# Graph layers on one Trainium2 core: 64x64 graph matrices, made a round ahead, and the values product in four quadrants

## What is computed

```python
# layer 0: attention, 8 heads of 64
attn = softmax(q @ k.T / 8) * 0.33 + 0.33 * adj + 0.33 * exp(-adj)      # masked
x = layernorm(x + (attn @ v) @ W_out + b_out)
# layer 1: mean over neighbours
agg = (adj @ x) / max(deg, 1e-6)
x = layernorm(x + relu(concat([x, agg]) @ W.T))
# layer 2: hypergraph convolution, twice, with H = (adj != 0)
Dn = 1 / (H @ adj[0]);  Be = 1 / H.sum(0)                               # 0 where the sum is not > 0
G = Dn * (H @ (Be * H.T));  h = layernorm(relu(G @ x @ W1.T + b1)) * gamma + beta
x = layernorm(x + G @ (h @ W2.T) + b2 + x)
# layer 3: gated attention
xg = x * sigmoid(deg * Wd + bd);  QK = sigmoid(xg @ Wqk.T + bqk)
s = (QK @ QK.T) / 16 * adj;  s = s / (s.sum(-1) + 1e-6)
x = layernorm(x + relu(s @ xg @ Wl.T + bl + xg @ Wr.T))
```

## Time and profile before

| | us |
|---|---|
| median of 3 runs (range) | 1361.08 (1360.6 to 1361.57) |
| the profiled execution, its own time | 1359.72 |
| its span, first to last instruction | 1357.9 |
| TensorE matmul busy | 1243.5 (92%), 11728 instructions |
| TensorE weight loads busy | 1074.6 (79%) |
| VectorE busy | 959.6 (71%), 2115 instructions |
| ScalarE busy | 551.9 (41%), 1058 instructions |
| GpSimd busy | 499.2 (37%), 633 instructions |
| granted TensorE clock, mean | 0.986 of full |

### The profile page before, as it was taken

One profiled execution on the slowest core, in us unless ns is written; L12 is line 12 of the kernel. 1 busy time (PEld: TensorE's weight loads), 2 busy tenths in 40 slices (PEclk: granted clock), 3 DMA queues, 4 the chain that ended last, 5 costly groups with the idle time before them and its releaser, 6 DMA issues.

```text
span 1357.9 us, 30718 instructions
## 1 busy us (share of the span) xinstructions
PE 1243.5 (92%) x11728; PEld 1074.6 (79%) x11728; DVE 959.6 (71%) x2115; ACT 551.9 (41%) x1058; POOL 499.2 (37%) x633
## 2 busy tenths in 40 slices
PE   5699999999999999999999999999999999999776
PEld 4578888788888878887888888878888887888665
DVE  4787676777767677776777777677776767777653
ACT  2344353443534344353444435344353534335221
POOL 2325252442624234261433525244262424425130
PEclk9899999999999999999999999999999999999897
DMA  6000101001010100101010010100101010010000
GB/s 199 21 20 21 36 2 40 15 19 35 11 44 0 39 15 19 35 0 39 15 39 15 19 35 0 39 15 20 34 19 35 0 39 19 0 36 2 20 1 16
DMA packets 43873, 34.93 MB, mean 26 GB/s; under 512 B 19319, under 2 KB 38717, under 8 KB 43838
## 3 DMA queue, kind: packets, MB, share of 16 engines
q1 hardware_dynamic: 43112, 34.04, 8.1%
q10 hardware_dynamic: 726, 0.40, 0.2%
HBM read 26.05 MB, written 8.39 MB: 25 GB/s over the span
## 4 chain that ended last, share of the span: by engine, by line
PE 63%; DVE 22%; issue 9%; ACT 4%; DMA 1%; DVEq 0%; POOL 0%; SPq 0%; ACTq 0%; POOLq 0%
PE bank L891 15%; PE bank L892 14%; PE bank L893 14%; PE bank L1067 5%; DVE x L681 4%; DVE hT_lo L605 3%; PE bank L984 3%; PE bank L959 3%; PE bank L1125 2%; DVE stats L670 2%; PE bank L1011 2%; PE bank L887 2%; DVE smax L713 2%; DVE x L822 2%; DVE yw L833 1%
## 5 line engine op out<-in xcount | busy, mean ns | idle before, releaser
L411 POOL TENSOR_SCALAR var<-mv 128x2 f32<-128x2 f32 (+1 forms) x192 | 42.5, 221 | 683.0 <-DVE mv L674 683.0
L681 DVE TENSOR_SCALAR x<-x,mv,rstd 128x256 f32<-128x256 f32 x256 | 129.7, 553 | 30.0 <-POOL rstd L414 29.9
L503 ACT ACTIVATE hT_hi<-bank 128x512 fp32r<-128x512 f32 x160 | 88.7, 600 | 142.6 <-PE bank L1011 116.2
L414 POOL TENSOR_TENSOR rstd<-var,negh 128x2 f32<-128x2 f32 (+1 forms) x192 | 127.1, 662 | 16.0
L605 DVE TENSOR_TENSOR hT_lo<-bank,hT_hi 128x512 fp32r<-128x512 f32 x160 | 102.9, 683 | 35.0 <-ACT hT_hi L503 30.6
L515 ACT ACTIVATE v<-bank 64x256 f32<-64x256 f32 x256 | 96.8, 378 | 56.5 <-PE bank L893 53.5
L670 DVE BATCH_NORM_STATS2 stats<-x 128x6 f32<-128x256 f32 x256 | 96.4, 419 | 4.4
L520 ACT ACTIVATE prob<-prob 128x512 f32<-128x512 f32 x64 | 40.5, 633 | 127.7 <-DVE prob L715 127.7
L456 POOL TENSOR_TENSOR prob<-prob,srec 128x512 f32<-128x512 f32 x64 | 66.8, 1044 | 65.5 <-DVE srec L723 65.5
L503 ACT ACTIVATE qT<-bank 128x512 f32<-128x512 f32 x64 | 38.3, 598 | 129.0 <-PE bank L893 129.0
L670 DVE BATCH_NORM_STATS2 stats<-r 128x6 f32<-128x512 f32 x64 | 44.5, 695 | 57.2 <-ACT r L503 57.2
(11 more groups left out here) (206 smaller groups left out, 3932.9 us busy)
## 6 DMA issues: line engine op xcount, KB each, us to landing
xTin<-in_x_t SPq DMA_DIRECT2D x32, 256.0 KB, 2.9
xin<-in_x SPq DMA_DIRECT2D x16, 512.0 KB, 3.7
out_x<-x SPq DMA_DIRECT2D x32, 256.0 KB, 2.3
adjA<-in_adj SPq DMA_DIRECT2D x16, 128.0 KB, 2.7
adjB<-in_adj SPq DMA_DIRECT2D x32, 64.0 KB, 3.0
r<-in_wqkv SPq DMA_DIRECT2D x2, 512.0 KB, 9.1
x<-in_wqkv SPq DMA_DIRECT2D x1, 512.0 KB, 10.7
x<-in_w_out SPq DMA_DIRECT2D x1, 512.0 KB, 11.0
```

The costliest lines, as they stand in the source:

```text
L414: pool.tensor_tensor(rstd[layer][:, lo:hi], var[layer][:, lo:hi], negh[:, lo:hi], ALU.pow).then_inc(SEM[f"rstd{n}"], 1)
L503: act.activation(dst, src[:, :], func, **kw).then_inc(SEM[ready], 1)
L681: ins = dve.tensor_scalar(x[:, t, :], x[:, t, :], mv[layer][:, t, 0:1], rstd[layer][:, t:t + 1], ALU.subtract, ALU.mult)
```

## The change

- The graph matrices are compact: 128 partitions (two graphs) x 4 tiles x 64 columns, half the elements, no zeros. adj is loaded as such, its transpose (adjAt, made ahead of the launch) and the first row of each graph spread over its partitions (wrow) too. Products on them are made in 64x64 squares (or 64 rows x 128 columns in `gathered`), one for each half of the partitions; `gathered` now makes both chunks in one step and fills both banks together, ordered by half.
- hT comes from adjAt by a comparison on VectorE; the counts and Dn's sums are reductions on VectorE. TensorE's graph_a and graph_b and ScalarE's graph_a are gone. The three transposes of the graph matrices and turn_s are products with the identity (`flipped`).
- All graph steps are now stream A's, in the middle and late part of the round, for the group that B takes up in the next round.
- pv takes two tiles in one step: even head pairs go straight into one bank, odd head pairs crosswise into the other, so that all four quadrants are used. W_out's rows are laid out to match.
- The banks are dealt out anew by the same rule.

```diff
-    ("B", "turn1", 0), ("B", "turn1", 1), ("A", "k", 1), ("B", "graph_a", 0), ("C", "scale3", 0), ("A", "k", 2),
+    ("B", "turn1", 0), ("B", "turn1", 1), ("A", "k", 1), ("C", "scale3", 0), ("A", "k", 2), ("A", "mask", 0),
...
-                    sp.wait_ge(*count("meanA_ready", b, 1, 1))
                     sp.wait_ge(*count("sim_ready", b, 1, 1))
-                    for h in range(2):
-                        sp.dma_start(adjB[h * N:(h + 1) * N, :, h * N:(h + 1) * N],
-                                     adj_h[b, h]).then_inc(SEM["adjB_in"], 16)
+                    sp.dma_start(adjB[:, :, :], adj_g[b]).then_inc(SEM["adjB_in"], 16)
...
             def graph_a(g, i):
 
-                dve.wait_ge(*count("adjB_in", g, 32))
-                dve.tensor_scalar(edge[:, :, :], adjB[:, :, :], 0.0, None, ALU.not_equal).then_inc(SEM["edge_ready"], 1)
-                dve.tensor_reduce(deg[:, :], adjB[:, :, :], AX.X, ALU.add).then_inc(SEM["deg_ready"], 1)
+                dve.wait_ge(*count("adjA_in", g, 16))
+                dve.wait_ge(*count("z_ready", g, 1, 1))
+                dve.tensor_reduce(deg[:, :], adjA[:, :, :], AX.X, ALU.add).then_inc(SEM["deg_ready"], 1)
+                dve.wait_ge(*count("adjAt_in", g, 16))
+                dve.tensor_scalar(hT0[:, :, :], adjAt[:, :, :], 0.0, None, ALU.not_equal).then_inc(SEM["ht_ready"], 1)
                 dve.wait_ge(*count("deg_ready", g, 1))
                 dve.tensor_scalar(degm[:, :], deg[:, :], 1e-6, None, ALU.max).then_inc(SEM["degmax"], 1)
+                dve.wait_ge(*count("ht_ready", g, 1))
+                dve.tensor_reduce(cnt[:, :], hT0[:, :, :], AX.X, ALU.add).then_inc(SEM["cnt"], 1)
...
             def graph_b(g, i):
...
+                dve.wait_ge(*count("cnt", g, 1))
+                dve.tensor_scalar(cntm[:, :], cnt[:, :], 1.0, None, ALU.max).then_inc(SEM["cntmax"], 1)
+                dve.wait_ge(*count("wrow_in", g, 32))
+                dve.scalar_tensor_tensor(out=edgew[:, :, :], in0=adjA[:, :, :], scalar=0.0, in1=wrow[:, :, :],
+                                         op0=ALU.not_equal, op1=ALU.mult).then_inc(SEM["edgew"], 1)
                 dve.wait_ge(*count("cntmax", g, 1))
                 dve.reciprocal(be[:, :], cntm[:, :]).then_inc(SEM["be_ready"], 1)
+                dve.wait_ge(*count("edgew", g, 1))
+                dve.tensor_reduce(dsum[:, :], edgew[:, :, :], AX.X, ALU.add).then_inc(SEM["dsum"], 1)
...
             def pv(g, i):
-                pe.wait_ge(*count("pT_ready", g, i + 1))
-                pe.wait_ge(*count("v_ready", g, i + 1))
...
+                if i % 2:
+                    return
+                pe.wait_ge(*count("pT_ready", g, i + 2))
+                pe.wait_ge(*count("v_ready", g, i + 2))
+                for odd in range(2):
+                    pe.wait_ge(*emptied("oT", i + odd, g))
+                    apart(pe, g)
+                ins = [None, None]
+                for k in range(2):
+                    for pair in range(HP // 2):
+                        for gr in range(2):
+                            for odd in range(2):
+                                p = 2 * pair + odd
+                                col = (pair * 2 + k) * P + gr * N
+                                for e in range(2):
+                                    rows, to = slice(e * N, (e + 1) * N), (e + odd) % 2
+                                    ins[odd] = pe.matmul(bank_of("oT", i + odd)[to * N:(to + 1) * N, col:col + N],
+                                                         v[rows, i + k, gr, p, :], pT[rows, k, p, gr * N:(gr + 1) * N],
+                                                         start=True, stop=True, skip_group_check=True)
...
+            def flipped(name, g, src):
+
+                pe.wait_ge(*emptied(name, 0, g))
+                dst = bank_of(name, 0)
+                apart(pe, g)
                 for t in range(T):
+                    for h in range(2):
+                        ins = pe.matmul(dst[square(h), t * N:(t + 1) * N], src[square(h), t, :],
+                                        ident[square(h), square(h)], start=True, stop=True, skip_group_check=True)
+                now_full(ins, name, 0)
...
+            def gathered(name, g, src, mat, halves=None):
+
+
+                ins = [None, None]
+                for c in range(C):
+                    for t in range(T):
+                        if halves and c == 0 and t % 2 == 0:
+                            pe.wait_ge(*count(halves, g, t // 2 + 1))
+                        at = slice((c * T + t) * N, (c * T + t + 1) * N)
+                        for h in range(2):
+                            if c == 0 and t == 0:
+                                pe.wait_ge(*emptied(name, h, g))
+                            ins[h] = pe.matmul(bank_of(name, h)[:, at], src[square(h), t, c * P:(c + 1) * P],
+                                               mat[square(h), t, :], start=True, stop=True, skip_group_check=True)
+                for h in range(2):
+                    now_full(ins[h], name, h)
...
                 now_full(product(dst[:, :], [(tile_of(spT, c, i), chunk(w1, c)) for c in range(C)], (0, HID),
-                                 [count("spread_lo", g, c + 1) for c in range(C)]), "up", i)
+                                 [count("spread_lo", g, 2)] * C), "up", i)
```

More of the change, by code:

```diff
@@ L89 @@
     "mixmat": "mm_ready", "q": "q_ready", "k": "k_ready", "v": "v_ready", "pT": "pT_ready", "oT": "oT_lo",
-    "out0": "sum0_ready", "turn1": "turn1_lo", "agg": "agg_lo", "mean": "sum1_ready", "ht": "ht_ready",
-    "cnt": "dsum", "sym": "g_ready", "meanT": "meanT_ready", "gT": "gT_ready", "spread": "spread_lo",
+    "out0": "sum0_ready", "turn1": "turn1_lo", "agg": "agg_lo", "mean": "sum1_ready", "sym": "g_ready", "meanT": "meanT_ready", "gT": "gT_ready", "spread": "spread_lo",
     "up": "relu_ready", "turn_h": "hT_lo", "down": "down_ready", "hyper": "sum2_ready", "turn3": "turn3_lo",
@@ L184, in graph_layers, with two @@
         rdeg = sb("rdeg", [P, T])
[L185 to L189 removed]
+        def two(name):
+            pair = sb(name, [P, 2, T, N])
+            return pair, pair[:, 0], pair[:, 1]
+        pair_m, meanA, meanT = two("mean")
+        pair_h, hT0, bhT = two("hyperedge")
+        cnt = sb("cnt", [P, T])
         cntm = sb("cntm", [P, T])
+        be = sb("be", [P, T])
         dsum = sb("dsum", [P, T])
[L192 to L194 removed]
         dsafe = sb("dsafe", [P, T])
@@ L211, in graph_layers @@
         xg = yw
-        sim = hT0
+        pair_s, sim, sT = two("sim")
         smat = sim
-        sT = bhT
+        lend = sb("lend", [P, 2 * HID + P])
         simsum = sb("simsum", [P, T])
@@ L282, in filled @@
             n = g * PER_BANK[b] + (c + 1 - back * PER_BANK[b])
-            return (zero_ready, 4) if isinstance(n, int) and n <= 0 else (full[b], n)
+            return (zero_ready, 2) if isinstance(n, int) and n <= 0 else (full[b], n)
         def emptied(fill, i, g):
@@ L642, in other_weights @@
                 if i == 2:
-                    three_parts([row0p[:, :, k] for k in range(3)], row0, gmat[:, 0, 0:T * GRP],
-                                gT[:, 0, 0:T * GRP])
                     dve.wait_ge(t_full, 1)
@@ L1054, in graph_d @@
-                dst = bank_of("gT", 0)
-                for t in range(T):
-                    ins = pe.transpose(dst[:, t * P:(t + 1) * P], gmat[:, t, :], ident[:, :])
-                now_full(ins, "gT", 0)
-            def gathered(name, g, i, src, mat, halves=None):
-                pe.wait_ge(*emptied(name, i, g))
-                dst = bank_of(name, i)
-                for t in range(T):
-                    if halves and i == 0 and t % 2 == 0:
-                        pe.wait_ge(*count(halves, g, t // 2 + 1))
-                    ins = pe.matmul(dst[:, t * P:(t + 1) * P], src[:, t, i * P:(i + 1) * P], mat[:, t, :],
-                                    start=True, stop=True)
-                now_full(ins, name, i)
+                flipped("gT", g, gmat)
@@ L1121, in simi @@
                 dst = bank_of("sim", 0)
+                apart(pe, g)
                 for t in range(T):
                     for c in range(C):
-                        tile = qkT[:, c, t * P:(t + 1) * P]
-                        ins = pe.matmul(dst[:, t * P:(t + 1) * P], tile, tile, start=(c == 0), stop=(c == C - 1))
+                        for h in range(2):
+                            one = qkT[:, c, t * P + h * N:t * P + (h + 1) * N]
+                            ins = pe.matmul(dst[square(h), t * N:(t + 1) * N], one, one, start=(c == 0),
+                                            stop=(c == C - 1), skip_group_check=True)
                 now_full(ins, "sim", 0)
@@ L1143, in out3 @@
                           + [(tile_of(agg3, c, t), chunk(wlr, c)) for c in range(C)], (HID + D, HID + 2 * D),
-                          [count("agg3_lo", g, c + 1) for c in range(C)])
+                          [count("agg3_lo", g, 2)] * C)
             steps = {
```

242 lines of the change are left out of this document (106 added, 136 removed), and 23 rows, old and new, of the table SCHEDULE.

## The result

The changed kernel takes 1544.66 us (median of 4 runs, 1541.84 to 1545.36), the kernel before 1360.84 beside it: ratio 1.1347, 95% interval 1.1327 to 1.1367. It is slower by 184 us. The direction was forecast, the size (+67) was not, and 1545 lies far outside the range of 1370 to 1455.

A forecast was written before the change was run, and what follows sets the result against it. TensorE is busiest, but VectorE, partly delayed by GpSimd, sets parts of the round. Dependence adds 2.0 us and the low clock 2.9: 14 x 4.9 = 69; with the ends, 1359.7 + 68 = 1428 us, range 1370 to 1455.

The forecast's parts named there:

- The first stretch: Round start to turn_h: mask product 4.1 us earlier, at 7.9; turn_h at 31.5 instead of 35.6.
- the prediction's 1.76: Gather agg3 at the round's end: 32 instructions take 1.76 us, counted equal to now (1.7).
- the load row: Trace row for weight loads: 192 ns for 128 columns, 137 for 64; used against faster gathers.
- The middle and pv 0: From turn_h to yw: hT0 waits for GpSimd's gate sum; TensorE stops 4.1 us, pv 0 at 44.15 against 44.41.
- the rivals: At the gate sum, VectorE's comparison goes first: with later scalings too, 1333 us, chance 0.12; alone, 1382 us, chance 0.1.
- the rival with the bank rule: At pv, two row halves may not write one bank: pv 0 stays at 2.2 us; 1443 us, chance 0.07.
- The wait before q 0: q 0 waits for norm0's first residual sum: starts at 60.05 against 57.50, a new stop of 2.55 us.
- clock term: Low clock behind the stops before pv 0 and q 0: 1.5 us each, 2.9 a round, bounds 0 and 5.2.
- the step "Sum": Whole program: 14 rounds x 4.9 = 69, plus the ends, from 1359.7 to 1428 us.
- the rival in which the clock costs more: Both low-clock stretches are long, 5.2 us a round instead of 2.9: 1460 us, chance 0.04.

The follow-up runs named there:

- e1: The changed kernel with 32 semaphore increments nobody waits for, once on TensorE ahead of its first round: 1472.52 us.
- e13: The changed kernel with 32 increments ahead of the loop, and graph_a moved two places, behind the second maxima: 1408.86 us.
- e3: The changed kernel with 32 increments ahead of the loop, and norm0's first residual sum moved earlier on VectorE: 1425.06 us.
- e5: The changed kernel with 32 increments ahead of the loop, the early residual sum and the early graph steps: 1332.62 us.
- e14: The changed kernel with early residual sum, early graph steps and early split of x, without increments ahead of the loop: 1358.29 us.
- e12: The changed kernel with 32 increments ahead of the loop, early residual sum, early graph steps and early split of x: 1288.88 us.
- e2: The changed kernel with 160 semaphore increments on TensorE ahead of the loop: 1496.6 us.

## Why the prediction was right or wrong

**The first stretch: right.** In e1, counted from the first transpose of turn1 (695.80), the mask product comes at 7.9 us (forecast 7.9) and turn_h at 32.1 (31.5, where the forecast's own terms give 31.4). Some 0.4 of the 0.6 are two gathers: from a gather's first start to the start of what follows it there are now 1.94 us (716.28 to 718.22 in the changed kernel), where there were 1.70 to 1.78; agg3 is the third. From first start to last start the 32 instructions take 1.73 us, as the prediction's 1.76 said (before 1.67 for 16), and the rest of the 1.94 lies between the gather and what follows. The load of 128 columns does not get faster with half the rows, as the load row said: 188 to 202 ns on average for the three gathers, 192 to 209 before.

**The middle and pv 0: right.** pv 0 comes at 44.8 (forecast 44.15) with the stop of 3.9 us released by pT's copy (4.1), and hT0 takes 2.25 us and ends with the gate sum. Who goes first at that place is settled against the rivals: 2123 ns in the changed kernel, 284 where GpSimd is idle (e13). pv at 18 ns an instruction (64 in 1.16 us at full clock) writes each bank from both row halves, so the rival with the bank rule falls.

**The wait before q 0: right in kind and place.** It is 2.3 us by sum0, and it goes with the early sum (e3). q 0 comes at 63.3 in e1, where the forecast with its clock term says 60.05 + 1.4 = 61.45. Half of the difference is before yw's end (58.3 for 56.1 + 1.4), half behind it, where turn3's transposes run at the low clock (1.54 us for six, 0.88 in the changed kernel). yw's end in e1, timeline of VectorE:

```profile
753.43 0.69 DVE L846 SCALAR_TENSOR_TENSOR yw<-r,x 128x512 f32<-128x512 f32 x1
```

**The clock: the right mechanism, mis-sized.** I put 3 us of work at the low level behind each of two stops, 2.9 us a round. Behind pv 0 that held (740.59 to 743.72). Around q 0 it did not: in e1 the level is low from 753.96 to 764.20, where the stop before turn3's second half (2.25 us) comes first and q 0's own stop follows. That is 10.2 us, of which some 7.7 are work (the last 0.3 us of this stretch are at the full clock again):

```profile
754.20:764.50 10.30, 8.01 (x35) 6.38 (x36) 4.22 (x9) 2.68 (x6) 0.93 (x2) 0.51 0.32 89
```

(windows view of e1). In all e1 has 13.7 us a round at the low level, some 11 of them work; by e5's rounds (1.5 us for each 3.4) that is 4.8 us a round, not 2.9. My bounds (0 to 5.2) held it. With it and the three gathers (0.6) the forecast of 85.3 becomes 87.8, against 88.7 measured; where the other 0.9 lie I did not find out.

**What failed: the step "Sum", which had no term for the code.** I counted the added matmuls only by what they take to run, and the compact products add 204 traced TensorE instructions to a round of 1468. From e1's 88.7 to the changed kernel's 93 to 95 there are 5 us a round, 72 us in all: the stops of 1.43 and 2.37 us, and the low clock behind them (729.82 to 733.23 in the round shown). I had no row of it, since the kernel before fetches nothing in its loop; the page's line of 24 packets with a loop of six blocks was there to be read, and was not.

The account against the forecast of 1428: 72 us by the code (e1) and 45 by the rest (1472.5 less 1428), together the 117 us that were missing. Of the 45, some 27 are the clock term (14 rounds of 4.8 less 2.9), 8 the gathers, and 10 are open. So the code alone does not explain the miss: without its effect the time is 1472.5, still above the end of the range (1455) and above the rival in which the clock costs more (1460). The clock term of 2.9 us a round was too small for that kernel too.

## What to carry to other kernels

Count the instructions of a loop's body on each engine before and after an edit, and look at the packets of the instruction queue: if their number grows with the passes of the loop, a few instructions ahead of the loop can be worth as much as a step inside it (here 72 us, or 5%; moving the graph steps gave 78). A change that takes work off an engine which is not what is late shows nothing until the stops are gone; here the same four quadrants were worth 0 and then 20 to 28 us. And look up what GpSimd runs at the place to which a VectorE instruction from SBUF to SBUF is moved: the same comparison took 284 ns beside an idle GpSimd and 2123 ns on average beside the gate sum.

## What the runs showed of the hardware that I had not expected

- A loop of 1672 traced TensorE instructions (and some 60 others) is fetched again at each of its 12 jumps back or never, by where its first instruction stands: 135 packets or 27. The difference is 72 us (e1) and 69 us (e14 to e12).
- Refetching by itself is nearly free where the second stop at the head is gone (e2: 88.9 us in the typical round with 135 packets, 88.7 with 27).
- 128 instructions more at the program's start let TensorE begin 16.4 us later (28.49 for 12.04). Not settled.
- A gather of half-height products side by side, each with 128 loaded and 64 moving columns, is no faster than the full-height one: 32 instructions keep TensorE for 1.94 us, the 16 before for 1.70 to 1.78.
